# A two-layer conditional kernel: first weights ahead on SyncE's queue, and expert transfers moved from the last step of a group to its first

## The reference, cut to what matters

```python
# x: (64, 128, 512) f32; itok_B_0_63: category of each of 64 batches; itok_B_0_15: expert of each
x = x + (einsum('bsd,bdh->bsh', x, W[cat]) + b[cat][:, None, :])        # layer 0, W: (64, 512, 512)
h = gelu(einsum('bnd,hd->bnh', x, fc1_w) + fc1_b)                       # 2048 hidden
shared = einsum('bnh,sh->bns', h, fc2_w) + fc2_b                        # 384 columns
expert = einsum('bnh,bph->bnp', h, experts_w[idx]) + experts_b[idx]     # 128 columns, idx: 16 experts
x = x + concatenate([shared, expert], axis=-1)
```

## Time and profile before

| | |
|---|---|
| median of 3 runs | 1657.6 us (1655.45 to 1658.23) |
| the profiled execution | 1657.96 us |
| its span, first to last instruction | 1656.2 us |
| mean granted clock of PE | 0.995 of full speed |
| busy: PE, DVE, ACT, POOL | 1637.2, 1314.8, 554.1, 214.4 us |
| moved | 243.44 MB, mean 147 GB/s |

### The profile page before, as it was taken

One profiled execution on the slowest core, in us unless ns is written; L12 is line 12 of the kernel. 1 busy time (PEld: TensorE's weight loads), 2 busy tenths in 40 slices (PEclk: granted clock), 3 DMA queues, 4 the chain that ended last, 5 costly groups with the idle time before them and its releaser, 6 DMA issues.

```text
span 1656.2 us, 27997 instructions
## 1 busy us (share of the span) xinstructions
PE 1637.2 (99%) x7064; PEld 1320.6 (80%) x7064; DVE 1314.8 (79%) x2004; ACT 554.1 (33%) x926; POOL 214.4 (13%) x195
## 2 busy tenths in 40 slices
PE   7999999999999999999999999999999999999999
PEld 4788887888888888888888888888888887888887
DVE  5787978788787887877878788787878878788865
ACT  4343333333333333333333333333333333333321
POOL 0110200202020120200202011020200202002100
PEclk8899999999999999999999999999999999999999
DMA  7665555546465454664546555454654546555410
GB/s 218 175 187 136 164 151 155 144 139 167 130 175 145 143 157 115 174 161 142 153 115 183 146 161 142 141 159 133 168 157 135 152 114 180 162 144 148 134 52 26
DMA packets 303178, 243.44 MB, mean 147 GB/s; under 512 B 34152, under 2 KB 234984, under 8 KB 303084
## 3 DMA queue, kind: packets, MB, share of 16 engines
q1 hardware_dynamic: 255852, 203.75, 45.1%
q10 hardware_dynamic: 47232, 38.82, 7.7%
HBM read 209.93 MB, written 32.51 MB: 146 GB/s over the span
## 4 chain that ended last, share of the span: by engine, by line
PE 97%; issue 1%; SPq 1%; DMA 1%; DVE 1%; ACT 0%; DVEq 0%
PE ps_out L812 42%; PE ps_e L797 21%; PE ps_h L797 21%; PE ps_y L784 10%; PE ps_t L745 1%; PE ps_h L784 0%; SPq L316 0%; DMA x_blocks<-in_x 0%; DMA e_blocks<-in_L_cond_W 0%; DMA exps<-in_itok_B 0%; SPq L348 0%; PE ps_e L745 0%; PE ps_h L782 0%; DVE w_split L602 0%; DVE y L637 0%
## 5 line engine op out<-in xcount | busy, mean ns | idle before, releaser
L812 PE MATMUL ps_out<-w2e,h 128*128 128x512 f32 x3072 | 756.6, 395 | 0.0
L812 PEld LDWEIGHTS ps_out<-w2e,h 128*128 128x128 f32 x3072 | 575.5, 188 | 137.8
L797 PE MATMUL ps_e<-y_t,w 128*128 128x512 f32 x1536 | 378.2, 396 | 0.5 <-DVE y_t L602 0.5
L797 PE MATMUL ps_h<-y_t,w 128*128 128x512 f32 x1536 | 376.4, 394 | 0.0
L797 PEld LDWEIGHTS ps_e<-y_t,w 128*128 128x128 f32 x1536 | 289.1, 189 | 68.9 <-issue 3.8
L797 PEld LDWEIGHTS ps_h<-y_t,w 128*128 128x128 f32 x1536 | 289.6, 189 | 65.3
L646 DVE STREAM_TRANSPOSE e_whole<-e_blocks 128x512 f32<-128x512 f32 x256 | 279.1, 1090 | 0.0
L528 ACT CAST w2e<-e_whole 128x512 fp32r<-128x512 f32 x256 | 158.7, 620 | 355.3 <-DVE e_whole L646 355.3
L671 DVE CAST h<-g_raw 128x512 fp32r<-128x512 f32 x256 | 125.6, 491 | 182.8 <-ACT g_raw L542 182.7
L461 POOL TENSOR_TENSOR x_raw<-x_raw,b_all 128x512 f32<-128x512 f32 x60 | 87.3, 1455 | 1286.3 <-DMA x_raw<-in_x 1238.5
L497 ACT CAST w_split<-w_raw 128x512 fp32r<-128x512 f32 x244 | 145.2, 619 | 213.3 <-DMA w_raw<-in_L_cond_W 122.5
(11 more groups left out here) (68 smaller groups left out, 459.3 us busy)
## 6 DMA issues: line engine op xcount, KB each, us to landing
e_blocks<-in_L_cond_experts_w SPq DMA_DIRECT2D x1024, 64.0 KB, 2.5
w_raw<-in_L_cond_W SPq DMA_DIRECT2D x248, 256.0 KB, 4.0
out<-resid SPq DMA_DIRECT2D x64, 256.0 KB, 2.6
b_all<-in_L_cond_b SPq DMA_DIRECT2D x60, 256.0 KB, 4.2
x_raw<-in_x SPq DMA_DIRECT2D x60, 256.0 KB, 4.7
x_blocks<-in_x SPq DMA_DIRECT2D x240, 64.0 KB, 3.2
y_rows<-y ACTq DMA_DIRECT2D x60, 256.0 KB, 3.5
x_blocks<-y_rows ACTq DMA_DIRECT2D x240, 64.0 KB, 2.7
```

The source lines that it names most:

```text
L797: last = nc.tensor.matmul(h_bank(c)[:, :], w1[:, w, k, c * P:(c + 1) * P], y_t[:, a, k, :, :].rearrange("p b s -> p (b s)"), start=(k == 0 ...
L812: last = nc.tensor.matmul(ps_out[b][:, :], h[:, c % 2, a, b * S:(b + 1) * S], fc2_columns(c, c % 2, w, b), start=(c == 0 and n == 0), stop ...
```

## The change

First stage. SP issues the category and the expert table and then weights at once: slices 0 to 3 one by one, the others in pairs, one 512 KB transfer for two slices, each with a semaphore of its own (`FIRST_W`). The bias row and the next batch's x follow the fourth slice of a batch. The experts' indices are read only behind all weights. ACT issues the x of batch 0, the first prep tile and the fc1 bias; prep tiles 1, 2 and 3 follow ACT's casts of slice 0, slice 1 and slice 4.

Step 0 of group 0. ACT and DVE work tile t = 5 (`prep_high`, `prep_low`) ahead of the gelu and its high part.

Every group. Step 15 issues no experts; step 0 issues batches 0 and 1 of quad 1, eight transfers. The expert bias rows are issued in step 11. The expert indices of a group are read after the x blocks of step 0, not at its start.

```diff
+    FIRST_W = ((0,), (1,), (2,), (3,), (4, 5), (6, 7), (8, 9), (10, 11), (12, 13), (14, 15))
...
+            def load_first_w(n, cat):
+
+                j, m = FIRST_W[n][0], len(FIRST_W[n])
+                after(sp, w_lo, j + m - W0SLOTS)
+                k, slot = j % KD, j % W0SLOTS
+                dst = w_raw[:, slot:slot + m, :] if slot < WSLOTS + 2 else e_blocks[:, 1, slot - WSLOTS - 2:slot - WSLOTS - 2 + m, :]
+                src = l0_w[bass.ds(cat, 1), :, :].rearrange("o (p k) n -> (o p) (k n)", k=KD)[:, k * D:(k + m) * D]
+                sp.dma_start(dst.rearrange("p k n -> p (k n)"), src).then_inc(w0_in[n], 16)
...
-            load_first_x(0)
+            sp.dma_start(exps[:, :], exp_ids.rearrange("(o n) -> o n", o=1)).then_inc(exps_in, 16)
             sp.wait_ge(cats_in, 16)
-            first_experts = []
-            for j in range(NC):
-                if j % KD == 0:
-                    cat = category(0, j // KD)
-                load_w(0, j, cat)
...
+            for n, slices in enumerate(FIRST_W):
+                b = slices[0] // KD
+                if slices[0] % KD == 0:
+                    cat = category(0, b)
+                load_first_w(n, cat)
+                if slices[-1] % KD == KD - 1:
+                    sp.dma_start(b0_rows[:, b, :], l0_b[bass.ds(cat, 1), :]).then_inc(b0_rows_in[b], 16)
+                    if b + 1 < GB:
+                        load_first_x(b + 1)
+            sp.wait_ge(exps_in, 16)
+            first_experts = [index(exps, b, exp_w.shape[0]) for b in range(GB)]
             load_experts(0, 0, first_experts, range(GB))
-            load_experts(0, 1, first_experts, [0])
...
                     if quad < NC // QUAD:
-                        load_experts(g, quad, idx, [b])
-                    elif more:
-                        if b == 0 and quad == NC // QUAD:
+                        load_experts(g, quad, idx, [0, 1] if c == 0 else [b])
+                    elif more and quad == NC // QUAD:
+                        if b == 0:
                             next_idx = [index(exps, (g + 1) * GB + i, exp_w.shape[0]) for i in range(GB)]
-                        load_experts(g + 1, quad - NC // QUAD, next_idx, [b])
+                            load_expert_bias(g + 1, next_idx)
+                        load_experts(g + 1, 0, next_idx, [b])
...
-            for t in range(PSLOTS):
-                load_prep(act, t)
+            act.dma_start(resid[:, 0, :], x[0, :, :]).then_inc(first_x_in[0], 16)
+            load_prep(act, 0)
...
+                    if c == 0:
+                        prep_high(prep_in_step(g, c, 0))
                     gelu(g, c)
-                    for n in range(PREP_RATE):
+                    for n in range(1 if c == 0 else 0, PREP_RATE):
                         prep_high(prep_in_step(g, c, n))
...
+                    if c == 0:
+                        prep_low(prep_in_step(g, c, 0))
                     h_high(g, c)
-                    prep_low(prep_in_step(g, c, 0))
+                    if c > 0:
+                        prep_low(prep_in_step(g, c, 0))
                     h_low(g, c)
```

More of the change, by code:

```diff
@@ L115, in build @@
         prep_in = [sem(f"prep_in{i}") for i in range(PSLOTS)]
-        w0_in = [sem(f"w0_in{i}") for i in range(W0SLOTS)]
+        w0_in = [sem(f"w0_in{i}") for i in range(len(FIRST_W))]
         w_in = [sem(f"w_in{i}") for i in range(WSLOTS)]
@@ L427, in body @@
                         load_l0_in(g + 1, c)
+                    if c == 0:
+                        idx = first_experts if first(g) else [index(exps, g * GB + b, exp_w.shape[0]) for b in range(GB)]
                     b, quad = (c + 1) % GB, (c + 1) // QUAD + 1
                     if quad < NC // QUAD:
-                        load_experts(g, quad, idx, [b])
-                    elif more:
-                        if b == 0 and quad == NC // QUAD:
+                        load_experts(g, quad, idx, [0, 1] if c == 0 else [b])
+                    elif more and quad == NC // QUAD:
+                        if b == 0:
                             next_idx = [index(exps, (g + 1) * GB + i, exp_w.shape[0]) for i in range(GB)]
-                        load_experts(g + 1, quad - NC // QUAD, next_idx, [b])
+                            load_expert_bias(g + 1, next_idx)
+                        load_experts(g + 1, 0, next_idx, [b])
                     if c == 0 and not first(g):
@@ L440, in body @@
                         load_expert_bias(0, first_experts)
-                    if more and c == NC - 1:
-                        load_expert_bias(g + 1, next_idx)
                 if not more:
@@ L492, in w_high @@
                 if first(G):
-                    act.wait_ge(w0_in[j % W0SLOTS], 16 * (j // W0SLOTS + 1))
+                    act.wait_ge(w0_in[[j in slices for slices in FIRST_W].index(True)], 16)
                 else:
@@ L535, in prep_high @@
                 nc.scalar.copy(prep_dst(t, 0), four(prep_bank(t))).then_inc(prep_hi, 1)
-                for u in prep_later(t):
-                    load_prep(act, u)
+                if t > 0:
+                    for u in prep_later(t):
+                        load_prep(act, u)
             def gelu(g, c):
@@ L553, in _ @@
                 w_high(0, j)
+                if j + 1 < PSLOTS:
+                    load_prep(act, j + 1)
             for j in range(NC):
```

29 lines of the change are left out of this document (8 added, 21 removed).

## The result

| | before | after |
|---|---|---|
| median | 1655.40 us (1653.23 to 1660.23, 20 runs) | 1659.01 us (1655.70 to 1661.43, 20 runs) |
| ratio | | 1.0018, 95% interval 1.0012 to 1.0024 |
| the profiled execution, its span | 1657.96, 1656.2 us | 1661.01, 1659.2 us |
| busy: PE, DVE | 1637.2, 1314.8 us | 1639.1, 1326.2 us |

What follows compares the result with a forecast made beforehand. PE was taken to bound the loop (busy 100.08 of 100.20 us), leaving gain mainly in the first stage and step 0. 4.5 + 3.5 + 0.35 = 8.35 us off 1657.96 gave 1649.6, median 1649.3, range 1645.0 to 1654.5.

Steps and rivals of the forecast that it cites:

- The groups: Loop groups: moving experts and bias rows was to gain 0, as PE has no gap there to close.
- rival D: Group's end: POOL's addition to an early x slows DVE's subtraction, PE stalls 0.9 us in 14 groups; 1661.5 us, chance 0.06.
- All that PE waits for comes earlier or at the same time ... gain 0: Loop groups: SP turns the loop early, stores come some 6 us earlier, yet PE has no gap to close.
- First stage: Start to slice 8: weights issued ahead bring slice 8 to 23.3 instead of 27.84 us, a gain of 4.5 us.
- I take 11 to 12, near the full rate: First stage: landing time in us of weight slices 4 and 5, between bounds of 10.5 and 15; before 16.25.
- rival C: First stage: bytes bind, late prep tiles hold PE's turns, low clock can return; gain 4.3 to 6 us, 1652.5, chance 0.18.
- Step 0: Group 0, first fc1 to first fc2: tile 5 split early removes a 2.02 us pause; gain 3.5 us.
- the 0.36 us named: Step 0 of group 0: tile 6, split behind the gelu, is late next; 0.3 us may be waited.
- The 0.35 us gap: Last group, at 1377 us: PE's gap where SP was late out of the loop goes, a gain of 0.35 us.
- Group 0: First fc2 to group 1: moved expert and bias loads have some 15 us to spare and cost nothing.
- rival E: Steps 1 to 3 of group 0: late prep tile or x blocks give the stage's gain back; 1657 us, chance 0.07.

Runs made afterwards that it cites:

- e4: The changed kernel with POOL's addition to a group's first x held until DVE has made step 0's low part: 1651.33 us, 0.9974 of before.
- e8: The kernel before with the new step-0 order, the groups' part and the held addition, but the old first stage: 1652.73 us, 0.9981 of before.
- e2: The kernel before with prep tile 5 split ahead of the gelu in step 0, nothing else: 1653.83 us, 0.9983 of before.
- e5: e3 with two unused index reads in SP's first stage, which shift the loop's code by 6 instructions: 1657.03 us, 1.0007 of before.
- e1: The kernel before with the groups' part of the change alone (experts and bias rows moved): 1659.66 us, 1.0023 of before.
- e12: The kernel before with 36 unused index reads on SP in group 0, ahead of the unchanged loop: 1678.36 us, 1.0151 of before.
- e3: The kernel before with the new first stage alone, step-0 order and groups as before: 1680.56 us, 1.0148 of before.
- e7: e4 with SP also waiting until PE has turned the last y before issuing the next group's weights: 1652.41 us, 0.9979 of before.
- e6: e4 with prep tiles 1 and 2 issued by ACT at the start, as before the change: 1650.88 us, 0.9967 of before.
- e9: e4 with 24 turns of the identity into an unused bank in PE's idle time at the start: 1652.71 us, 0.9985 of before.

## Why the prediction was wrong

**The groups (forecast 0; measured a loss of 7.7 to 8.3 us, given back by e4).** The failed step is the threshold in rival D: "It decides when x lands later than about 5.6 us after issue", with "0.6 us of room" over the median landing of 4.8. Two of its terms were wrong.

The larger one is the moment of the issue. I had x issued 6.37 us ahead of the cast (1151.2, the cast at 1157.57). In the trace after it is 3.0 to 5.5 us ahead, 4.5 at the median of the 13 ends of groups at which such an addition falls. In the group shown above it is 4.82, later than forecast by 1.55 us, of which 0.5 lie between the first weights and x (2.06 us instead of 1.55; the 0.36 us of the block edge at position 15 are among them) and the rest is spread over the last experts and the turn of the loop. With 4.5 us and an addition of 1.3, even the subtraction alone, 0.46 us behind the cast, is met by every landing over 3.6 us, and the landings took 3.8 to 5.2. The second term is the operation that can be met first. I counted only the subtraction of h, which starts at 1158.04, and left out the cast right ahead of it, at 1157.57; that makes the threshold 5.0 instead of 5.6 even with the issue as forecast. The trace after shows the cast held as well, 1.51 us instead of 0.43.

Where I saw room there was none: six of the 14 groups lost 0.9 to 1.1 us between the cast and `fc1`, two more 0.7 and 0.3, and D had a chance of 0.06. Its price for a group hit, 0.9 us, was right; "14 groups, 12.6 us" was too many. That D's time, 4 us slower, is close to the 3.6 measured is chance: D sets 12.6 lost against 8.35 gained, and it was 8.3 against 4.7. The Trainium skill would have shown the second mistake: SBUF — State Buffer, Who interferes with whom, names casts among the DVE operations that can take the port pair it shares with GpSimd, and the 1.51 us agree. I had cited its neighbouring section for the subtraction alone.

**"All that PE waits for comes earlier or at the same time ... gain 0"** was perhaps read too narrowly in the other direction as well. With the addition held, the groups' move looks like a small gain, which the times don't hold apart from nothing: e8, which has it, is 1.5 us faster than e2, which doesn't, by the medians, and 0.3 us by the ratios (0.9981 and 0.9983). In the traces the 14 groups took 1403.34, 1405.76 and 1406.19 us with the old order (before, e2, e5), 1402.19 to 1404.61 with the new one and the hold (seven traces). I had read one group of the loop, where PE was busy throughout; in before others take 0.3 to 0.6 us longer, and in e2 they lose 0.3 to 0.8 us to late x blocks.

**First stage (forecast 4.5; measured 0.6 in the trace, about 1 by e4 against e8).** The issue times of the first slices were right. Two things were not. "I take 11 to 12, near the full rate" for the pair's landing: it came at 13.6, between that and the bound by the stage's rate (15), and prep tile 1 landed at 13.7 and held PE; that was rival C's mechanism, "prep tiles 1 and 2 now start later ... and can hold PE's turns, and the low clock can come back". The low clock did not so much come back as stay, up to 24.3 us. And I measured the gain against one trace whose stage ended later than in any other of its kind. `fc1(0, 0)` starts in the five traces with the old stage at 41.63, 41.13, 39.45, 39.31 and 38.67 us (before, e2, e1, e8, e12), in five with the new one at 41.04, 40.12, 39.34, 38.03 and 37.12 (after, e5, e3, e7, e4). The means are 40.0 and 39.1: a gain of 0.9 in a spread of 4. e4 gave just what was forecast, slice 8 at 23.6 and `fc1(0, 0)` at 37.1, and the kernel after, with the same stage, neither. What differs is the low clock. Ahead of slice 8 PE had it for 15.3, 16.1, 18.7, 19.4 and 24.3 us in e4, e7, e3, e5 and after, in the very order in which `fc1(0, 0)` came later. With the old stage the order is not so clean (11.8, 19.0, 21.2, 21.6 and 21.6 us in e12, before, e8, e1 and e2). The low-clock stretch lies differently in each execution; I forecast the lucky one, and the 4.5 us were mis-sized by it.

**Step 0 (forecast 3.5; 3.8 in the trace, 2.2 in e2's time).** The pause went and nothing took its place but the 0.36 us named. Part of its size was again the trace I started from: `fc1(0, 0)` to `fc2(0, 0)` took 12.49 us in it, and 8.97 to 11.93 in the four others with the old order (10.8 us in the mean of the five); with the new one 7.09 to 9.57 (8.1 in the mean of nine). The term was mis-sized by about 1 us; its mechanism held.

**The 0.35 us gap** of the last group went, as forecast.

**Group 0 (forecast 0; +1.1 us).** From `fc2(0, 0)` to group 1 the traces take 105.9 to 109.9 us with either order. One to three waits ahead of a prep tile's turn, most of them of 1.1 to 1.5 us (0.3 to 2.4), recur in all of them, the kernel before included. They resemble what rival E describes, but they were there before the change; what sets their number I did not settle.

**The sum**, by medians, each difference uncertain by 1 to 2 us: e4, the change without the collision, is 4.7 us faster than before, of which the step gives 2.2 (e2), the groups' move 1.5 (e8 to e2) and the stage 1.0 (e4 to e8); the last two can't be told from nothing. The collision takes 8.3 back. So the forecast of 8.35 was too high by 3.7 even where everything went as meant, and the rest of the miss, 8.3, is rival D. The kernel to keep is the changed one with the held addition, e4 or e6: 0.9974 and 0.9967 of before.

What remains open: e6 and the fill of e9 together weren't tried, nor a stage with the prep tiles' bytes moved behind the weights.

## What to carry to other kernels

When a queue runs earlier, follow each transfer to the engine that acts on its landing, and lay that operation over every operation of the neighbour it can hold, casts included, not only over the one that feeds the bottleneck. Work that has slack should be made to wait for the moment when it does no harm; one semaphore was worth some 8 us. Lay an issue time that comes from a sum of small pieces over the neighbour's operations with the error of the sum, here 1.5 us, not as a point. Read a short stage from several executions before its microseconds are put into a sum, and after any edit of the code ahead of a loop, look for pauses at the loop's head before the edit is judged.

## What the runs showed of the hardware that was not expected

- **SP's code position.** With one loop body, the time was 1656 or 1678 us by where the loop lies among blocks of 128 instructions. Each block edge costs SP 0.34 to 0.38 us, each turn at the branch 2.4 to 4.2 us, and an edge three instructions behind the loop's head a further 1.4 to 1.7 us. That position is the cause is shown by e5 and e12; that the pauses go with fetches of code, by the packets on the queue of instructions (82 in before and e5, 95 and 96 in e3 and e12).
- **POOL against DVE.** An addition of 1.3 us on POOL with both inputs in SBUF made a DVE cast of 0.43 us take up to 1.57 us, and a subtraction of 0.69 us up to 1.79. When POOL ended 0.01 us ahead of the cast, nothing was lost, and a DVE transpose beside the addition kept its 1.1 us. With the addition held (e4), casts took 0.43 us and subtractions 0.69 again.
- **TensorE's pace at the start.** Ahead of the trace's first clock record (24.27 us in after, 6.25 in e9) the clock column reads 1.00, while matmuls ran at the pace of 1.2 GHz, 1.28 us for three of 512 columns instead of 0.70. Keeping PE at work from 1.5 us on brought slices 0 and 1 to full pace; a wait of 2.87 us took it away again.
